# The mask of the local scores: from a matmul on PE to DVE's maximum, in a fused attention and feed-forward layer

## The reference

```
y  = layernorm(x);  q, k, v = y@Wq, y@Wk, y@Wv     32 query heads, 8 key heads, 128 wide; gate g = k
o_lin = gla_scan(softmax(q), softmax(k), v, log_sigmoid(g)/16)      gated linear attention
y_loc = sliding_window(rope(q), rope(k), v)        blocks of 64 queries, keys of this and the previous block,
                                                   masked to 0 <= distance <= 64 and key position >= 0, softmax
x  = x + layernorm(bf16(0.5*y_loc + 0.5*o_lin) @ Wo)
x  = x + layernorm((silu(h@dq1.T) * (h@dq2.T)) @ dq3.T),  h = layernorm(x)
dq = NF4 quantised and dequantised weight: blocks of 64, absmax, 16 levels
```

## Time and profile before

| | |
|---|---|
| median of 3 runs | 1970.0 us (1969.61 to 1970.91) |
| the profiled execution | 1971.56 us, its span in the trace 1969.8 us |
| busy, share of the span | PE 95%, PEld 64%, DVE 73%, ACT 64%, POOL 64% |
| mean granted PE clock | 0.985 of full speed; 1.00 from 100 to 1560 us |
| from 100 to 1560 us | attention and NF4 |

### The profile page before, as it was taken

How to read it: one execution, slowest core, us unless ns; L and a number is a source line. 1 busy time by engine, 2 the same in 40 slices (tenths; PEclk the granted TensorE clock), 3 DMA queues, 4 the chain that set the end, 5 groups by cost and what they waited for, 6 DMA issues and landing times. The chain is left out here.

```text
span 1969.8 us, 43595 instructions
## 1 busy us (share of the span) xinstructions
PE 1880.7 (95%) x11700; PEld 1259.0 (64%) x11700; DVE 1432.2 (73%) x3952; ACT 1252.7 (64%) x4898; POOL 1266.3 (64%) x1189
## 2 busy tenths in 40 slices
PE   2899999999999999999999999999999779999997
PEld 2577777677777777776777767777677545444443
DVE  7788888888888888888888888888888664302022
ACT  6577777777777777777777777777777555312121
POOL 4777777777777777777777777777777631212121
PEclk8999999999999999999999999999999989999999
DMA  5000000000000000100000000000000132000000
GB/s 181 28 31 24 24 24 24 29 29 24 24 24 24 24 24 24 32 24 24 24 24 29 24 24 24 24 29 29 24 24 24 68 116 80 23 0 22 0 21 21
DMA packets 47052, 63.87 MB, mean 32 GB/s; under 512 B 5232, under 2 KB 20080, under 8 KB 47024
## 3 DMA queue, kind: packets, MB, share of 16 engines
q1 hardware_dynamic: 47024, 63.52, 10.0%
HBM read 50.86 MB, written 12.65 MB: 32 GB/s over the span
## 5 line engine op out<-in xcount | busy, mean ns | idle before, releaser
L342 POOL TENSOR_TENSOR f_acc<-f_acc,f_s 128x512 f32<-128x512 f32 x416 | 530.8, 1276 | 26.1 <-POOL f_acc L342 0.5
L879 PE MATMUL bank<-wh,xh 128*128 (+1 forms) x1024 | 334.8, 327 | 6.0 <-POOL wl L330 4.2
L879 PE MATMUL bank<-wl,xh 128*128 (+1 forms) x1024 | 334.7, 327 | 0.0
L879 PE MATMUL bank<-wh,xl 128*128 (+1 forms) x1024 | 334.7, 327 | 0.0
L324 POOL TENSOR_TENSOR pr<-pr,rp 128x512 f32<-128x512 f32 x128 | 133.1, 1040 | 210.1 <-DVE rp L616 210.1
L1364 POOL TENSOR_TENSOR hl<-hf,hh 128x512 f16<-128x512 f32 (+1 forms) x44 | 50.8, 1154 | 288.3 <-ACT hh L1233 288.3
L682 DVE TENSOR_SCALAR f_s<-f_nrm 128x512 f32<-128x512 f32 x480 | 227.6, 533 | 4.4
L413 ACT ACTIVATE qe<-bank,nqm 128x128 f32<-128x128 f32 x512 | 180.8, 365 | 78.4 <-DVE qs L547 58.1
L441 ACT ACTIVATE pr<-bank,pmx 128x128 f32<-128x128 f32 x512 | 180.6, 366 | 39.0 <-DVE pmx L609 32.7
L868 PE MATMUL bank<-wh,oT 128*128 (+1 forms) x512 | 194.1, 379 | 2.5 <-ACT oT L482 2.5
L868 PE MATMUL bank<-wl,oT 128*128 (+1 forms) x512 | 194.0, 379 | 0.0
(11 more groups left out here) (181 smaller groups left out, 5150.1 us busy)
## 6 DMA issues: line engine op xcount, KB each, us to landing
raw_qkv<-wq SPq DMA_DIRECT2D x36, 256.0 KB, 2.4
raw_o<-wo SPq DMA_DIRECT2D x36, 256.0 KB, 2.6
f_raw<-wf SPq DMA_DIRECT2D x33, 256.0 KB, 2.7
dequantised<-f_dq SPq DMA_DIRECT2D x32, 256.0 KB, 2.0
wt<-dequantised SPq DMA_DIRECT2D x31, 256.0 KB, 2.9
rows<-x SPq DMA_DIRECT2D x4, 1024.0 KB, 8.6
xr<-x SPq DMA_DIRECT2D x16, 256.0 KB, 4.4
out<-yo SPq DMA_DIRECT2D x16, 256.0 KB, 2.0
```

The lines of the kernel that those rows point to most:

```text
L342: nc.gpsimd.tensor_tensor(f_acc[:], f_acc[:], f_s[:, k % 8, :], ALU.add).then_inc(s["f_ad"], 1)
L879: last = nc.tensor.matmul(dst, av, w[:, sl + c, lo:hi], start=(n == 0), stop=(n == 3 * NC - 1))
```

## The change

PE's mask matmul goes; the first of the four score matmuls now starts the bank. DVE's `p_max` becomes, for each of the four heads, a `tensor_tensor_reduce`: it computes -(SC + mask), writes that back to `SC` in PSUM, and reduces it by min to `pmx`, which so holds the same negated maximum. A memset of one element per partition stands in front of the four and takes the wait for the scores. ACT's exponential reads `SC` with a scale of -1. The mask's version for the first tile, of which only the first two heads' columns differ, is copied by ACT to `win0` in turn 0, and PE waits for that copy before the scores of a tile with `t.p` of 0.

```diff
+        gate = sb("gate", [P, 1])
+        win0 = sb("win0", [P, P], BF16)
...
+            def head_mask(t):
+
+                if t.p == 0:
+                    nc.scalar.activation(win0[:], win[:, t.i % 2, 0:P], ACT.Copy).then_inc(s["head_mask"], 1)
+
...
                     last = nc.scalar.activation(pr[:, r, j * P:(j + 1) * P], SC[:, j * P:(j + 1) * P], ACT.Exp,
-                                                bias=pmx[:, r, j:j + 1],
+                                                bias=pmx[:, r, j:j + 1], scale=-1.0,
                                                 accum_out=psm[:, r, j:j + 1])
...
                     k_exps(t)
                     nf4_abs(t)
+                    head_mask(t)
...
             def p_max(t):
                 r = t.p % 2
                 wait_tile(dve, s["sc_done"], t)
-                nc.vector.tensor_reduce(pmx[:, r, :], SC[:].rearrange("p (h n) -> p h n", h=GRP), AX.X, ALU.max,
-                                        negate=True).then_inc(s["pmx_d"], 1)
+                nc.vector.memset(gate[:], 0.0)
+                for j in range(GRP):
+                    sl = slice(j * P, (j + 1) * P)
+                    mask = win[:, 1, sl] if t.p or j >= 2 else win0[:]
+                    last = nc.vector.tensor_tensor_reduce(SC[:, sl], SC[:, sl], mask, -1.0, -MASKED, ALU.add,
+                                                          ALU.min, pmx[:, r, j:j + 1])
+                last.then_inc(s["pmx_d"], 1)
...
                 wait_tile(pe, s["p_exp"], t, 1)
-                nc.tensor.matmul(SC[:], identb[:], win[:, 1, :] if t.p else win[:, t.i % 2, :], start=True, stop=False)
+                if t.p == 0:
+                    pe.wait_ge(s["head_mask"], t.i + 1)
...
-                                                start=False, stop=(j == 3))
+                                                start=(j == 0), stop=(j == 3))
```

More of the change, by code:

```diff
@@ L221, in attention @@
             x_st x_mv x_var x_sd x_rs x_shift x_norm x_turned x_hi x_lo zeroed id_in
-            f_in f_absd f_maxd f_safed f_recd f_nrmd f_sd f_ad f_dqd f_out f_rin f_rest f_rout""".split()
+            f_in f_absd f_maxd f_safed f_recd f_nrmd f_sd f_ad f_dqd f_out f_rin f_rest f_rout head_mask""".split()
         s = {n: sem("s_" + n) for n in names}
```

## The result

The changed kernel takes **1979.25 us** (median of 6 runs, 1978.64 to 1982.03), the kernel before 1970.01 us in the same job (6 runs, 1967.91 to 1970.91): a ratio of 1.0051, 95% interval 1.0039 to 1.0064. So it is slower by 9.2 us.

The account below looks back on a forecast made before the run. The prediction took DVE and POOL working by turns, not PE, as the bound: 1971.6 + 31 x 0.87 (27.0) = 1998.6 us, less 1.6 to the median, so 1997 us, range 1980 to 2014.

Parts of the forecast that it names:

- The ring of DVE and POOL: Path alternating between DVE and POOL, with turn 1's maximum on it, claimed to set the four-turn step of 46.81 us.
- 4 x 0.35 + 0.06 = 1.46 us, longer by 0.87: DVE's new maximum: four heads at 0.35 us plus a memset of 0.06, against 0.59 us for the old maximum.
- The first rival: DVE's accumulator read is not held: 0.26 us a head, maximum longer by 0.51, 1986 us; chance 0.24.
- the low bound of 0.51: Lower bound in us on the new maximum's lengthening on DVE, if the accumulator read does not wait.
- The sum: Loop body: 31 passages at 0.87 us give 27.0 us, added to the profiled 1971.6; median forecast 1997 us.
- I count 0 of the 28 us: PE's 128 saved bias matmuls at 0.22 us each were claimed to bring no time, only longer PE waits.
- In turn 0 DVE reached f_safe 0.9 us before POOL finished: Turn 0: DVE's wait at f_safe for POOL's addition was claimed to cover the maximum's lengthening of 0.87 us.
- Turns 2 and 3 covered: The 0.87 us lengthening there adds nothing a second time, since DVE's f_s still comes while a POOL addition runs.
- POOL's additions end 0.87 later too: Reason given for turns 2 and 3: POOL is delayed as much as DVE, so DVE's f_s still meets an addition.
- ACT's copy covered: ACT's 0.27 us mask copy in each step costs nothing, at most 8 us if it were not covered.
- should rise from 0.8 to about 2.6 us in a step: PE's total wait for kt and pr in each step, claimed to grow by about this much, with a step of 47.7 us.
- PE as the bound (1942): Rival: PE sets the time, so every saved bias matmul is won, 1970 - 28 = 1942 us; chance 0.10.

Follow-up runs that it names:

- e2: Changed kernel with the new maximum in turn 1 only; the other turns keep the mask matmul and old maximum: 1978.47 us, 1.0042 to the kernel before.
- e5: Kernel before with the old maximum (0.59 us of DVE) run a second time in turn 1: 1984.33 us, ratio 1.0072.
- e1: Kernel before without PE's mask matmul, the mask left out of the scores and DVE's maximum as before: 1947.1 us, ratio 0.9890.
- e15: Changed kernel with the low half of the log decay moved behind f_safe in turn 0: 1961.27 us, 0.9959 to the kernel before.
- e8: Kernel before with the old maximum (0.59 us of DVE) run a second time in turn 0: 1971.51 us, ratio 1.0006.
- e6: Kernel before with the old maximum (0.59 us of DVE) run a second time in turn 2: 1983.62 us, ratio 1.0066.
- e3: Changed kernel with the new maximum in turns 2, 3 and 0 only, the old one in turn 1: 1972.95 us, 1.0015 to the kernel before.
- e4: Changed kernel without ACT's mask copy and PE's wait for it, first tiles masked wrongly: 1981.62 us, 1.0056 to the kernel before.
- e10: Changed kernel with NF4 comparisons spread 3, 4, 4, 4 over turns 0 to 3, not 2, 4, 5, 4: 1949.45 us, 0.9891 to the kernel before.
- e14: Changed kernel with the old maximum and its mask matmul in turn 0 alone: 1978.77 us, 1.0049 to the kernel before.
- e16: Kernel before with the low half of the log decay moved behind f_safe in turn 0: 1955.73 us, ratio 0.9922.

## Why the prediction was right about the sign and wrong about the size

- **The ring of DVE and POOL, with turn 1's maximum on it: right.** e2 has nearly the whole loss in turn 1, and e5's dose of 0.59 lengthens the step by 0.52.
- **The step that failed: "4 x 0.35 + 0.06 = 1.46 us, longer by 0.87".** Measured are 0.96 and 0.37. I took the price of the read from ACT's pairs, where the read starts late and holds up the next instruction. DVE's read starts together with the next main instruction. The first rival, the read that is not held, was the right mechanism, and still too dear: it adds a whole slot of 0.06 for a read, and 0.06 for a memset, where together they cost less. So the low bound of 0.51 was no bound, and the range, although it began 6 us below that rival's 1986, still lay above the result. The Trainium skill (VectorE: DVE Perf Modes, "Two Vector instructions with no wait between them") counts main and read as two instructions that nothing holds here; the trace agrees, with equal starts at 1011.77, 1012.01 and 1012.26. Where the prediction sets the rows at 1005.01 against the Trainium skill (VectorE: DVE Perf Modes, "The DRAIN you can't avoid"), it reads only half of the paragraph: its end says that a next op that is not held starts earlier, and the rows agree with that.
- **The sum, with the size put right.** 31 x 0.37 = 11.5 us. Some 0.05 us per step came back between turn 1's maximum and turn 2's rotation of k: the first instruction there that reads PE's projection starts 0.60 us after qtT's start, where it was 0.65 before. That DVE had waited there for PE is inferred. This makes 31 x 0.32 = 9.9, and 9.2 were measured. The path was right; the term alone was mis-sized.
- **"I count 0 of the 28 us": right for this kernel, for a reason I had not seen.** I argued that POOL's additions end no earlier. e1 shows that the saved matmuls bring 23 us when the maximum does not grow: f_safe then comes before the last addition and need not wait for it. The changed kernel's arrival can be added up from the others: +0.33 before, -0.53 for the earlier PE (e1), +0.37 for the longer maximum = +0.17, and the trace has +0.16. e15 moves it to -0.18 and wins 18 us. So the change is slower by 9 us because of the ring, and f_safe is 0.16 us too late for a version that would be 18 us faster than it, 9 us below the kernel before.
- **"In turn 0 DVE reached f_safe 0.9 us before POOL finished", so covered: right**, and e8 shows it with a dose of 0.59. **Turns 2 and 3 covered: right for turn 2 only up to 0.13 us**, by e6; e3 leaves about 3 us for the three turns together. The argument that "POOL's additions end 0.87 later too" does not hold for a delay that begins in turn 2: POOL's start in that turn waits for the rotation of k, which stands in front of turn 2's maximum. What hid the new maximum there was PE's saved matmul, with the 0.13: "covered" came true for turn 2 by luck, not by the reason given.
- **ACT's copy covered: right** (e4). **PE's waits "should rise from 0.8 to about 2.6 us in a step": right but for the lengthening.** Four turns of 11.28 are 45.12, so PE waits 47.13 - 45.12 = 2.0 us, and 2.6 less the 0.5 of the lengthening that did not come is 2.1. But not all of it is in turn 1: 0.46 us stand before line 861 in turn 0, where DVE's qtT came late behind the comparisons of turn 3, which meet POOL's additions.
- **PE as the bound (1942): wrong for this kernel**, but e1 and e10 come within 5 and 7 us of it. A chance of 0.10 for it was not too high.

## What to carry to other kernels

Price an instruction by the distance between starts of its neighbours on the same engine; a pair on another engine is a poor stand-in, and where it is all there is, a low bound must let the second of a pair cost nothing. Where an engine waits for a resource that is held in turns, the wait is a staircase: look how far its start is from the last edge, for a shift of 0.2 us can be worth nothing or a whole wait, here 1.1 us of f_safe and 0.6 to 0.7 us of a step. Look also at what ties the two arrivals: here, once PE waited for qtT, both hung on its end, and a longer turn 1 or 2 moved neither against the other. Before calling saved work worthless, ask which waits it moves and over which edge.

## What the hardware showed that I had not expected

- **DVE's accumulator reads are nearly free here.** A read shows 0.14 us by duration and has an equal start with the next main instruction; it is 0.24 to 0.25 us for a 128x128 head with mask, minimum and write back to PSUM, against 0.20 for a plain tensor_tensor from start to start. ACT's read cost 0.09 us in the same kernel.
- **An f_safe or f_s of DVE that meets a running POOL addition waits for its end whole, but slips in between two.** Not every DVE instruction does: f_max, next to f_safe, takes 0.69 us beside the additions. POOL's additions start every 1.35 us and last 1.27. f_safe takes 0.17 us when it comes before the next one, and 0.38, 0.96, 1.03, 1.13 or 1.28 by how much of a running one is left. The Trainium skill (SBUF — State Buffer, "SBUF: two separate sides") calls the port pair of DVE and GpSimd an exclusive lock, held for its whole instruction by whichever comes first; on DVE's side it concerns an instruction with two SBUF inputs, as f_safe has, or one in a two-port mode. These durations agree with it.
- **The edge can make one program take two step times.** In e14 and e16 the step jumps by 0.6 to 0.7 us from one iteration to the next. The four runs of e16 spread over 0.6%; 14 late f_safe at 0.71 us each are 9.9 us, and the profiled execution, which has them, is 11.6 above the lowest. That the others had fewer is likely but not shown, as only one was profiled.
